# Keys in front of queries in the projection, the squares and the cosines, and the norms in two halves

## The reference

```python
h = shift_token(x)
q, k, v = split(h @ wqkv, 3)              # 8 heads of 64
q = l2norm(q) * qs                        # each head by the root of its sum of squares
k = l2norm(k) * ksc
q, k = rotary_xpos(q, k)                  # q * cos * scale + rotate_half(q) * sin * scale, k with 1 / scale
o = local_attention(q, k, v)              # windows of 128, each with the one before, masked softmax
x = x + o @ wo
h = layernorm(shift_token(x)) * lg + lb
a, g = split(h @ w1 + b1, 2)
x = x + (a * gelu(g)) @ w2 + b2
```

## Time and profile before

| what | value |
|---|---|
| median of 3 runs | 2883.49 us (2872.27 to 2885.71) |
| the profiled execution | 2884.1 us, its span 2882.3 us |
| TensorE busy | 2756.7 us, 96% of the span |
| VectorE, ScalarE, GpSimd busy | 80%, 75%, 38% |
| the second block | projections from 1533 us to 2816 us, some 20 us a step |

### The profile page before, as it was taken

One profiled execution on the slowest core, in us unless ns is written; L12 is line 12 of the kernel. 1 busy time (PEld: TensorE's weight loads), 2 busy tenths in 40 slices (PEclk: granted clock), 3 DMA queues, 4 the chain that ended last, 5 costly groups with the idle time before them and its releaser, 6 DMA issues. The chain is left out here.

```text
span 2882.3 us, 60204 instructions
## 1 busy us (share of the span) xinstructions
PE 2756.7 (96%) x22992; PEld 1750.5 (61%) x22992; DVE 2315.0 (80%) x4287; ACT 2151.2 (75%) x4620; POOL 1086.3 (38%) x1179
## 2 busy tenths in 40 slices
PE   7999999999999999999997899999999999999997
PEld 7733333333333333333346788888888888888886
DVE  6769999999999999999917677777777777777774
ACT  5558888888888888888875566776666677777764
POOL 7600000010001000010007566666666666777664
PEclk9969999999999999999999899999999999999999
DMA  5603243434442443344312100000001100000000
GB/s 166 190 17 48 42 61 55 64 56 75 62 71 53 73 62 66 57 74 64 70 32 102 40 5 7 6 7 7 5 7 58 68 14 19 21 20 15 21 19 25
DMA packets 92637, 138.74 MB, mean 48 GB/s; under 512 B 38528, under 2 KB 63040, under 8 KB 84928
## 3 DMA queue, kind: packets, MB, share of 16 engines
q1 hardware_dynamic: 86416, 125.40, 21.8%
q10 hardware_dynamic: 5936, 9.50, 1.0%
HBM read 88.17 MB, written 37.75 MB: 44 GB/s over the span
## 5 line engine op out<-in xcount | busy, mean ns | idle before, releaser
L684 ACT ACTIVATE probs<-scores 128x512 f32<-128x512 f32 x2048 | 1114.4, 597 | 210.4 <-PE scores L610 88.4
L717 DVE TENSOR_REDUCE mx<-aux 128x1 f32<-128x1024 f32 x982 | 1200.7, 1223 | 72.6 <-PE aux L578 65.3
L578 PE MATMUL aux<-k_stack,q_stack 48*128 48x512 f32 x2006 | 754.9, 452 | 13.6 <-DVE mx L725 8.1
L610 PE MATMUL scores<-q_stack,k_stack 50*128 50x512 f32 x2048 | 767.5, 453 | 0.0
L623 PE MATMUL pv<-probs,v_ones 128*32 128x256 f32 x8192 | 663.3, 396 | 0.1
L610 PEld LDWEIGHTS scores<-q_stack,k_stack 50*128 50x128 f32 x2048 | 312.6, 187 | 433.2 <-ACT probs L684 415.6
L623 PEld LDWEIGHTS pv<-probs,v_ones 128*32 128x32 f32 x8192 | 162.1, 108 | 364.3 <-ACT probs L684 286.5
L531 POOL CAST m_parts<-head_max 128x16 fp32r<-128x16 f32 x32 | 6.3, 196 | 887.7 <-DVE head_max L710 887.7
L578 PEld LDWEIGHTS aux<-k_stack,q_stack 48*128 48x128 f32 x2006 | 304.5, 188 | 42.4 <-DVE mx L717 18.0
L1461 ACT ACTIVATE VO<-VO,tables_small 128x256 f32<-128x256 f32 (+1 forms) x512 | 250.6, 491 | 42.3 <-DVE tables_small L1630 41.9
L1305 PE MATMUL bank<-q_minus_first,q_stack 128*128 128x256 f32 x2112 | 270.3, 286 | 2.2 <-POOL q_minus_first L1093 2.2
(11 more groups left out here) (178 smaller groups left out, 4512.7 us busy)
## 6 DMA issues: line engine op xcount, KB each, us to landing
q_stack<-qk_dram SPq DMA_DIRECT2D x192, 128.0 KB, 5.4
k_stack<-qk_dram SPq DMA_DIRECT2D x192, 128.0 KB, 7.1
qk_dram<-qkT_hi SPq DMA_DIRECT2D x32, 256.0 KB, 3.5
qk_dram<-qkT_lo SPq DMA_DIRECT2D x32, 256.0 KB, 3.9
w_parts<-weight_pieces SPq DMA_DIRECT2D x28, 256.0 KB, 2.4
VO<-o_stage SPq DMA_DIRECT2D x128, 32.0 KB, 6.9
q_minus_first<-sums_dram SPq DMA_DIRECT2D x32, 128.0 KB, 3.0
x_dram<-x_sb SPq DMA_DIRECT2D x16, 256.0 KB, 2.0
```

What stands on the lines that cost most here:

```text
L578: return nc.tensor.matmul(out, q_stack[max_rows, n % BODY, tile * P:(tile + 1) * P], k_stack[max_rows, n % BODY, keys * 512:(keys + 1) * 512],
L610: last = nc.tensor.matmul(out, k_stack[0:SCORE_ROWS, n % BODY, s * P:(s + 1) * P], q_stack[0:SCORE_ROWS, n % BODY, j * 512:(j + 1) * 512], ...
L684: nc.scalar.activation(probs[:, e % PROBS], scores[:, item_of_exp(e) % BANKS1], ACT.Exp, scale=float(D1) ** -0.5).then_inc(act_emptied, 1)
L717: nc.vector.tensor_reduce(mx[:, n % BODY, tile, half:half + 1], aux[:, unit % 2].rearrange("p a k -> p (a k)"), AX.X, ALU.max).then_inc(dv ...
```

## The change

KEYS_FIRST = (1, 0, 2) sets the order of the projection and of the ScalarE copies and squares: keys, queries, values. The cosines follow in the same order. The sum of squares (square_norms) becomes two instructions of 8 norms each: the keys' half stands between the two cosines, the queries' half where the whole stood. inverse_norms becomes two floors and two powers of 8 columns, keys first. scale_keys waits for the first power alone, and the next step's first mask_and_maximum has a new wait for the second. In transposed_probs group 2 now waits for both squares and both cosines, group 3 for the first of each.

The diff:

```diff
--- before.py
+++ after.py
@@ -757,6 +757,7 @@
 
 
 LOW_BEHIND = 3
+KEYS_FIRST = (1, 0, 2)
 LAYERS = 2
 H2, D2 = 8, 64
 INNER = H2 * D2
@@ -1077,10 +1078,11 @@
 
             def inverse_norms(v):
 
-                pool.wait_ge(norm2_made, v + 1)
-                nc.gpsimd.tensor_scalar(norm2_min, norm2, 1e-24, None, ALU.max).then_inc(norm2_floor, 1)
-                pool.wait_ge(norm2_floor, v + 1)
-                nc.gpsimd.tensor_tensor(out=rnorm[:, v % 2], in0=norm2_min, in1=minus_half, op=ALU.pow).then_inc(rnorm_made, 1)
+                for i, heads in enumerate((slice(H2, 2 * H2), slice(0, H2))):
+                    pool.wait_ge(norm2_made, 2 * v + i + 1)
+                    nc.gpsimd.tensor_scalar(norm2_min[:, heads], norm2[:, heads], 1e-24, None, ALU.max).then_inc(norm2_floor, 1)
+                    pool.wait_ge(norm2_floor, 2 * v + i + 1)
+                    nc.gpsimd.tensor_tensor(out=rnorm[:, v % 2, heads], in0=norm2_min[:, heads], in1=minus_half[:, heads], op=ALU.pow).then_inc(rnorm_made, 1)
 
             def split_y(v):
 
@@ -1197,7 +1199,7 @@
                 if v == NT:
                     pe.wait_ge(weights.wqkv1_loaded, 32)
                 hi, lo = wqkv_hi, wqkv_lo
-                for a in range(3):
+                for a in KEYS_FIRST:
                     if v:
                         pe.wait_ge(max_made, 4 * (v - 1) + a + 1)
                     columns = slice(a * INNER, (a + 1) * INNER)
@@ -1270,8 +1272,8 @@
                         else:
                             pe.wait_ge(o_normed, 2 * (PAIRS1 - 2))
                     if j >= 2 and exists(v + 1):
-                        pe.wait_ge(squares_made, 2 * (v + 1) + j - 1)
-                        pe.wait_ge(cos_done, 2 * (v + 1) + j - 1)
+                        pe.wait_ge(squares_made, 2 * (v + 1) + 4 - j)
+                        pe.wait_ge(cos_done, 2 * (v + 1) + 4 - j)
                     for u in range(2):
                         for kb in key_blocks(v):
                             last = nc.tensor.transpose(bank[PT_BANK[j]][:, (2 * u + kb) * P:(2 * u + kb + 1) * P], probs[j][:, u, kb * P:(kb + 1) * P], ident[:])
@@ -1464,8 +1466,8 @@
 
             def copy_projected(v):
 
-                for a in range(2):
-                    act.wait_ge(qkv_done, 3 * v + a + 1)
+                for i, a in enumerate(KEYS_FIRST[:2]):
+                    act.wait_ge(qkv_done, 3 * v + i + 1)
                     if v:
                         act.wait_ge(sin_made, v)
                         act.wait_ge(qkT_done, 2 * v)
@@ -1623,6 +1625,8 @@
             def mask_and_maximum(v, j):
 
                 dve.wait_ge(S_done, 4 * v + j + 1)
+                if j == 0:
+                    dve.wait_ge(rnorm_made, 2 * v + 2)
                 src, blocks = bank[S_BANK[j]], key_blocks(v)
                 n_keys, mask_at = P * len(blocks), P if len(blocks) == 1 or current(v) == 0 else 0
                 at = blocks[0] * P
@@ -1681,18 +1685,18 @@
 
             def cosines(v, a):
 
-                if a == 0:
+                if a == KEYS_FIRST[0]:
                     dve.wait_ge(tables_made, 2 * (v // 2 + 1))
-                dve.wait_ge(squares_made, 2 * v + a + 1)
+                dve.wait_ge(squares_made, 2 * v + 2 - a)
                 nc.vector.tensor_tensor(qk_cos[:, a].rearrange("p (h d) -> p h d", d=D2), bank[QKV_BANK[a]][:].rearrange("p (h d) -> p h d", d=D2),
                                         cos_table[:, v // 2 % 2, a].unsqueeze(1).to_broadcast([P, H2, D2]), ALU.mult).then_inc(cos_done, 1)
 
-            def square_norms(v):
-
-                dve.wait_ge(squares_made, 2 * v + 2)
+            def square_norms(v, a):
+
+                dve.wait_ge(squares_made, 2 * v + 2 - a)
                 if v:
-                    dve.wait_ge(norm2_floor, v)
-                nc.vector.tensor_reduce(norm2, squares.rearrange("p a (h d) -> p (a h) d", d=D2), AX.X, ALU.add).then_inc(norm2_made, 1)
+                    dve.wait_ge(norm2_floor, 2 * v - a)
+                nc.vector.tensor_reduce(norm2[:, a * H2:(a + 1) * H2], squares[:, a].rearrange("p (h d) -> p h d", d=D2), AX.X, ALU.add).then_inc(norm2_made, 1)
 
             def copy_PT(v, j):
 
@@ -1702,7 +1706,7 @@
 
             def rotate(v):
 
-                dve.wait_ge(norm2_made, v + 1)
+                dve.wait_ge(norm2_made, 2 * v + 2)
                 dve.wait_ge(cos_done, 2 * v + 2)
                 dve.wait_ge(sin_made, v + 1)
                 nc.vector.tensor_tensor(qk_rot[:, 0], qk_cos[:, 0], qk_sin[:, 0], ALU.add)
@@ -1711,7 +1715,7 @@
             def scale_keys(v):
 
                 dve.wait_ge(rot_made, v + 1)
-                dve.wait_ge(rnorm_made, v + 1)
+                dve.wait_ge(rnorm_made, 2 * v + 1)
                 nc.vector.tensor_tensor(qk_rot[:, 1].rearrange("p (h d) -> p h d", d=D2), qk_cos[:, 1].rearrange("p (h d) -> p h d", d=D2),
                                         rnorm[:, v % 2, H2:].unsqueeze(2).to_broadcast([P, H2, D2]), ALU.mult).then_inc(rotary_done, 1)
 
@@ -1789,9 +1793,10 @@
                 if k == 6:
                     split_xT(0)
                 if k == 10:
+                    cosines(0, 1)
                     cosines(0, 0)
-                    cosines(0, 1)
-                    square_norms(0)
+                    square_norms(0, 1)
+                    square_norms(0, 0)
                 if k == 11:
                     split_xT(1)
                 if k == 12:
@@ -1824,8 +1829,9 @@
                 if t == -1:
                     outputs_step(PAIRS1 + 2)
                 if exists(t + 2):
+                    cosines(t + 2, 1)
+                    square_norms(t + 2, 1)
                     cosines(t + 2, 0)
-                    cosines(t + 2, 1)
                 if t == -1:
                     outputs_step(PAIRS1 + 3)
                     outputs_step(PAIRS1 + 4)
@@ -1834,7 +1840,7 @@
                 if exists(t + 1):
                     copy_PT(t + 1, 1)
                 if exists(t + 2):
-                    square_norms(t + 2)
+                    square_norms(t + 2, 0)
                 if exists(t + 1):
                     copy_PT(t + 1, 3)
                 if finished is not None:
```

## The result

| | kernel before | changed kernel |
|---|---|---|
| median, timed side by side | 2879.2 us (20 runs) | 2864.4 us (20 runs) |
| ratio, 95% interval | 1 | 0.994 (0.9924 to 0.9957) |
| once more, on another occasion | 2877.4 us (21 runs) | 2864.1 us (10 runs), 0.9963 (0.9947 to 0.9979) |
| span of the profiled execution | 2882.3 us | 2862.7 us |

The account below looks back on a forecast made before the run. TensorE bounds the kernel, busy 2756.7 of 2882.3 us. Terms +1.3 (regular odd steps), -3.3 (three odd steps) and -7.2 (layers' beginnings) sum to -9.2 us; with the median 0.6 lower, 2874 us, range 2863 to 2884.

Parts of the forecast that it names:

- The regular odd step: Half sum delays second cosine, pushes normalisation L1680 behind GpSimd's second sine; gain eaten, 26 steps lose 0.05 us each, +1.3.
- the wait of L1255: Odd steps: besides the cosine wait, TensorE waits at L1253 (old line number) and the product behind it, together about 1.1 us.
- the main entry of the waits: TensorE's 34 waits at query and key transpositions for scaled keys, 41.5 us; forecast nearly gone, under 5 us.
- t = 3 and 37: Odd steps with L1680 already behind the sines: half sum hidden, 1.1 us won each, part of -3.3 us.
- t = 35: Third odd step with L1680 already behind the sines (1.52 us): 1.1 us won, part of -3.3 us.
- The even steps: Half sum of 0.60 us fits the 0.71 us of room between the cosines; L1680 and TensorE unmoved, zero.
- The second layer's beginning: Waits of 3.4 us at t = 31 and 32 go, less 0.2 us kept at t = 32 for the transposition.
- The first layer's beginning: Waits of 4.6 us at t = -1 and 0 go, less 0.6 us kept at t = -1 for the half sum.
- L1680 gets in all the same: Rival: normalisation still slips between the sines, regular odd steps win 0.24 us each; 2867 us, chance 0.17.
- the half sum doesn't fit into the even steps: Rival: L1680 falls behind the second sine, 0.57 us lost in each of 29 even steps; 2890 us, chance 0.14.
- the beginnings don't pay: Rival: other late transfers or maxima leave nothing of the 7.2 us at the layers' beginnings; 2881 us, chance 0.14.
- faster: Outcome of the measurement: whole kernel faster than 2869 us; chance 0.20.

Follow-up runs that it names:

- beginnings only: The change made only for windows 1, 2, 33 and 34, all others as in the kernel before; 2868.1 us, ratio 0.9965.
- halves only: Kernel before with sum, floor and power in halves, both half sums in the old place, queries in front elsewhere; 2833.4 us, ratio 0.9846; again 2839.1, 0.9837.

## Why the prediction was right and wrong

The regular odd step came out as written. The second cosine moved by 0.59 (0.60 predicted), the third group of transpositions started 0.15 behind it (0.16), its delay was 0.88 (0.86), and the normalisation was over 0.15 behind the sines and took 1.01 ("1.0 to 1.1"). TensorE's waits are 0.71 for the cosine and 0.15 for a copy; the wait of L1255 that was foreseen between them does not show. The sum's half is 0.67 us a piece, the power 1.7. So the main entry of the waits, 41.5 us, was indeed eaten up where the prediction put it, and the experiments show both parts of the reason: with the half sum out of the way 27 us come back, with shorter sines 12.6.

For the long stretch the prediction's terms make 5.2 us (3.3 + 3.2 - 1.3), and 5.1 were measured (means of four profiles). That agreement is partly luck, since terms of it were off and cancel. The lengths of the steps, from one transposition of queries and keys to the next, say:

- The 26 regular odd steps lost 0.02 us each, 0.4 in all, not 0.05 and 1.3.
- t = 3 and 37 won 1.3 and 1.2, as written; t = 35 won 0.3 in the mean, not 1.1, because the slow normalisation there was in the first profile alone, the one that the prediction read. The cause was different, too: beginnings only shows that t = 3 and 37 are mended without any half sum hidden behind their wait.
- The even steps stayed, as predicted, but for t = 10, which lost 0.55.

The second layer's beginning, 3.4 - 0.2 = 3.2 us, measured 3.3.

The first layer's beginning is the mis-sized term: the prediction took the two waits of the earlier trace rows, 4.6 us, less 0.6, so 4.0; measured are 7.4 in the mean, 4.1 to 10.6 by the pair that one takes. The two steps that it counted, t = -1 and 0, won 4.6. What it left out stands on either side of them. Up to the first transposition of queries and keys (t = -2) 1.1 us were won: window 0 has a wait of its own for the scaled keys, which ended before the window of the earlier trace rows begins and is the odd one of the 34 waits of the earlier trace rows:

```profile
1558.15 1.09 PE L1342 MATMUL bank<-ident,VO 128*128 128x128 f32 x8 [1.21 <-DVE VO L1715]
```

And t = 1, which the sum does not mention, won 2.0, though TensorE's idle time in it fell by only 0.4; t = 2 gave back 0.3 in the mean, all of it in one of the four profiles.

By kinds, TensorE's idle time in the whole piece fell from 30.5 to 26.2 us, so by 4.3, close to the 4.0. The other 3.1 us are busy time: the same 687 or 688 products took 122.5 us before and 119.4 in the changed kernel (means of four). Two things were not in the sum. First, some of the idle time was another wait: TensorE stood there for the copy of group 3 of the transposed probabilities, which VectorE makes behind the whole sum, and started 0.1 us behind that copy's end both times; the halved sum lets it go earlier. The trace lists it as "issue". Waits of TensorE, whole span, before and changed:

```profile
PE bank L1319 <- issue: 3.1, 2, 1.9
```

```profile
PE bank L1321 <- issue: 1.6, 2, 1.2
```

With the halves only, where both halves stand ahead of that copy, the same entry is 3.2. In the three other profiles of the changed kernel it is about 2.0. Second, TensorE's clock is low for part of these steps, for which the prediction had no term: 31 to 34 us in the four profiles of the kernel before, 20 to 27 in those of the changed kernel. That part also varies for one program (20 and 27 us with the halves only, and 4.7 us between the two beginnings), and with beginnings only it was 31 us without the two waits, in a beginning of 149.3 us, 3.7 under the mean of before. So the step that failed is the term for the first layer's beginning: it counted two waits, and put the first window's wait, the wait for the copy and the clock at nothing, 4.0 us where 7.4 came. How much of the 3.1 us of busy time belongs to the change stays open.

The rest of the distance between 2874 and 2864.4 is none of the kernel's: the forecast stood on the median of 3 runs, 2883.5, which became 2879.2 with 20 runs. With that and the 12.5 us of the trace one arrives at 2866.7. The last 2 us are within the first block's scatter.

Of the rivals, "L1680 gets in all the same" fell by the 1.01 us, "the half sum doesn't fit into the even steps" by the 0.43 (0.71 at t = 52, without a loss; t = 10 alone is as that rival said), and "the beginnings don't pay" by the beginnings only, with a ratio of 0.9965. The chance for "faster", 0.2, was too low: the intervals of both timings reach from under to over 0.5%.

## What to carry to other kernels

Cutting an instruction in two so that its first half's consumer starts sooner paid here only where the first half stood in nobody else's way: the same two halves were worth 35 us of the long stretch in the old place and nothing, in the regular steps, between the cosines. Before an instruction is put ahead of others, look at what every one of those others releases, and at which instruction of another engine it will then meet. To compare two profiles, cut them at rows that both have; pieces that no change touches show how much of a difference is chance. A step that a single profile shows can itself be chance, as t = 35 was, so a term that rests on one wants a second profile.

## What the runs showed of the hardware

One and the same normalisation on VectorE (128 x 256) took 0.40 to 0.44 us when it got in between two GpSimd instructions, 0.60 behind short ones, and 1.01, 1.20, 1.41 or 1.52 behind long ones. The reverse is seen on GpSimd with the halves only, t = 49: the same floor of 8 columns takes 0.24 us, and 0.74 when it starts while VectorE rotates (2540.45 to 2541.72). What the two engines share there was not tried.

```profile
2538.49 0.24 POOL L1082 TENSOR_SCALAR tables_small<-tables_small 128x8 f32<-128x8 f32 x1
...
2540.48 0.74 POOL L1082 TENSOR_SCALAR tables_small<-tables_small 128x8 f32<-128x8 f32 x1
```

In the first block TensorE's clock is low for 31 to 106 us, in stretches that differ between executions of the same program, and while TensorE is busy almost without a gap. Windows of the kernel before, first and third profile:

```profile
1060.00:1160.00 100.00, 98.09 (x932) 36.71 (x928) 94.97 (x84) 85.03 (x157) 4.93 (x10) 1.00 0.45 70
```

```profile
1060.00:1160.00 100.00, 98.92 (x766) 34.95 (x762) 78.23 (x70) 69.93 (x130) 4.92 (x10) 0.78 0.32 52
```

TensorE is busy for 98 and 99 of 100 us, but with 0.78 of the clock it does 766 products instead of 932. The six executions whose first block ended at 1499 us or later had 58 to 106 us at the lower level, the eleven others 31 to 65. What sets it off was not tried.
